# A four-layer graph transformer on one core: GpSimd issues the transfers of the inverse row sums

## Chip, cores and metric

The kernel runs on one core of one Trainium2 chip. The metric is the device time of one execution in microseconds (us); lower is better. Engines are called PE (TensorE), DVE (VectorE), ACT (ScalarE), POOL (GpSimd) and SP (the sync engine, which only issues transfers). DMA is a transfer between memories; it is issued by an instruction on SP or on POOL and ends, some time later, with a semaphore.

## What is computed

Four residual layers over `x` (8 batches, 1024 tokens, 256 features) and one adjacency matrix of 1024x1024. Layers 0 and 1 are graph convolutions. Layers 2 and 3 are attention with 8 heads of 32 features:

```python
# layer 2: mask is adj != 0; output projection, then o + layernorm(o)
attn = softmax(where(mask == 0, -inf, q @ k.T * scale))
o = (attn @ v) @ w_proj + b_proj
x = x + o + ln(o) * ln_gamma + ln_beta
# layer 3: (1 - adj) * -1e9 is added to the scores
attn = softmax(q @ k.T / sqrt(32) + (1 - adj) * -1e9)
x = x + (attn @ v) @ Wo + bo
```

`h = relu(layernorm(x))` feeds each layer. The kernel leaves the attention unnormalised until after the product with the values; only then does it multiply by the inverses of the row sums. Those inverses are what the change is about.

## The kernel before

**Phases.** `graph_phase` computes layers 0 and 1 (about the first 470 us). `attention_phase` computes layers 2 and 3: 16 jobs, one for each batch and layer (jobs 0 to 7 are layer 2, jobs 8 to 15 layer 3). A job has 64 units `u` (8 heads by 8 query tiles) and takes some 140 us. Each engine has a program of its own, written out by hand in the order in which the engine is to work; semaphores join them. While PE works on job n it also works off, in slots at fixed units, the end of job n-1 (table `EARLY`), the middle of job n (`MID`) and the beginning of job n+1 (`NEXT`).

**The four pairs of heads.** Two heads at a time share one output bank. For pair `pr` (0 to 3):

1. PE turns the row sums of 16 units (slot `norm`, L1047) and DVE takes their reciprocals into `rT`, 16x128 (L1399). The slots are at u=18, 33 and 48 for pairs 0, 1 and 2, and at u=1 of the following job for pair 3.
2. `write_rows` copies `rT` to the DRAM tensor `inverse_row_sums` (8 KB, L853). `read_rows` waits until that has landed and reads it back with 4 transfers, each repeated over 32 partitions, into `R_ot`, 128x512 (L859). Both are in SP's program. SP reaches them between `move_head` and `place_head` of heads 0, 2, 4 and 6: `move_head` sends a tile of probabilities to DRAM (L799) and `place_head` waits until it has landed and brings it back turned, with 4 transfers (L811).
3. ACT copies the output bank to `ot_sb` (L1260, semaphore `ot_done`).
4. POOL multiplies `ot_sb` by `R_ot` (`scale_ot`, L1656) once `ot_done` and `rows_in` say so, and issues 8 transfers to `oT_raw` (`regroup`, L1674).

**What follows on POOL.** POOL's program is `body` from L1718. Behind pair 3 of the job before come `move_v` (L1587), `bias_xe` (L1592) and `turn` (L1684, L1686), which splits a part of `oT_raw` for the output projection that PE does in the slots `out` at u=11, 15, 19 and 26 (L961 to L963 with `t_oT`). Behind `split(job, SPLITS[3])`, which follows the projection slot of u=22, come pair 0, then `bias_xe` of part 3 (needed by DVE's L1420 for the slot `out` 3 at u=26, in jobs 9 to 15 only), then `row_scale` (L1575, L1577, waits for the mean and variance that DVE makes in L1457), `norm` (L1623, L1626: four steps) and four splits of `h`. PE's slots `h` at u=34 and 35 (L1062) wait for `hn_done`, which L1626 counts: the one at u=34 for the second step, the one at u=35 for the fourth. Then come pair 1, `add_ln` of parts 2 and 3 (jobs 1 to 8), four splits, pair 2, and, in job 7 alone, `load_mask3` (L1712), which loads the mask of layer 3, needed by DVE's L1446.

Of the kernel before, what the change touches and what calls it, by code (L numbers as in the profile page):

```python
# [23 lines left out]
P = 128  # L24
# [512 lines left out]
def attention_phase(nc, a, x_mid, x_mid2, out, mask, shared, ident, PT, split, x_left, row_scratch, turned_rows, w_scratch):  # L537
# [11 lines left out]
    with ExitStack() as ctx:  # L549
# [199 lines left out]
        def _(sp):  # L749
# [95 lines left out]
            def write_rows(job, pr, key):  # L845

                pair = 4 * job + pr
                b, n = place[key]
                sp.wait_ge(bank_freed[b], n + 1)
                if pair:  # L850

                    sp.wait_ge(scaled, pair)
                sp.dma_start(row_scratch.rearrange("h (t q) -> (h t) q", q=P), rT[:]).then_inc(rows_out, 16)  # L853

            def read_rows(job, pr):

                sp.wait_ge(rows_out, 16 * (4 * job + pr + 1))
                for j in range(4):
                    sp.dma_start(R_ot[j * HD:(j + 1) * HD, :].rearrange("p (h t) -> p h t", h=2),  # L859
                                 row_scratch[:, 2 * j * P:2 * (j + 1) * P].partition_broadcast(HD)).then_inc(rows_in, 16)  # L860

            def body(job, layer, before, after):
                move_head(job, 0)
                if before is not None:
                    write_rows(job - 1, 3, key_of(job, ("norm", 3)))
                place_head(job, 0)
                if before is not None:
                    read_rows(job - 1, 3)
# [18 lines left out]
                write_rows(job, 0, key_of(job, ("norm", 0)))  # L887
                place_head(job, 2)
                read_rows(job, 0)
# [16 lines left out]
                write_rows(job, 1, key_of(job, ("norm", 1)))  # L906
                place_head(job, 4)
                read_rows(job, 1)
# [7 lines left out]
                write_rows(job, 2, key_of(job, ("norm", 2)))  # L916
                place_head(job, 6)
                read_rows(job, 2)
# [645 lines left out]
        def _(pool):  # L1564
# [85 lines left out]

            def scale_ot(job, pr):

                pair = 4 * job + pr
                pool.wait_ge(ot_done, pair + 1)
                pool.wait_ge(rows_in, 64 * (pair + 1))
                nc.gpsimd.tensor_tensor(ot_sb[:], ot_sb[:], R_ot[:], op=ALU.mult).then_inc(scaled, 1)  # L1656
# [61 lines left out]
            def body(job, layer, before, after):  # L1718
                if before is not None:
                    scale_ot(job - 1, 3)  # L1720
                    regroup(job - 1, 3)
# [20 lines left out]
                split(job, SPLITS[3])  # L1742
                scale_ot(job, 0)
# [5 lines left out]
                if after is not None:  # L1749
                    row_scale(job + 1)  # L1750
                    norm(job + 1)
                    for what in SPLITS[4:8]:
                        split(job, what)
                scale_ot(job, 1)
# [4 lines left out]
                if after is not None:  # L1759
                    for what in SPLITS[8:]:  # L1760
                        split(job, what)
                scale_ot(job, 2)
# [52 lines left out]
```

## Time and profile before

| | |
|---|---|
| median of 2 runs | 2754.8 us (2751.31 to 2758.28) |
| the profiled execution | 2757.91 us |
| its span, first to last instruction | 2756.0 us |
| granted TensorE clock, mean | 0.995 |
| PE busy | 2685.0 us, 97% of the span |
| DVE busy | 2238.5 us, 81% |
| ACT busy | 2022.5 us, 73% |
| POOL busy | 1384.9 us, 50% |
| DMA, mean over the span | 141 GB/s |

A busy time is the union of an engine's instructions. Idle time of an engine is put down to what ended it. The share says nothing of where a delay would hurt: an engine that is idle half the time can still be the one that another waits for at a given slot.

### The profile page before, as it was taken

To read this page: it belongs to the slowest core of one execution; us is meant where nothing else is said; L and a number is where in the kernel's file an instruction comes from. 1 tells how busy PE (TensorE), PEld (TensorE's weight loads), DVE (VectorE), ACT (ScalarE), POOL (GpSimd) and SP (SyncE) were. 2 spreads that over 40 slices of the span, in tenths; PEclk is the share of its full clock that TensorE was granted. 3 is DMA by queue.
4 is the path that set the end of the run, shared out by engine and by line. 5 is a ranking of instruction groups with operands and counts; after the bars stand their busy time and mean duration, and the time that the engine had idled before them with its cause. 6 is when DMAs were issued, how large, how long until landed. Compare 5 with 4: busy or idle time off the path is not lost.

```text
span 2756.0 us, 59363 instructions
## 1 busy us (share of the span) xinstructions
PE 2685.0 (97%) x22568; PEld 2113.3 (77%) x22568; DVE 2238.5 (81%) x4047; ACT 2022.5 (73%) x3680; POOL 1384.9 (50%) x1600
## 2 busy tenths in 40 slices
PE   9999999899999999999999999999999999999999
PEld 7888888677777777777777777777777777777776
DVE  6767676888888888888888888888888878887877
ACT  3000001888888888888888888888888888888887
POOL 2222221256767676767675758453535353536343
PEclk9999999999999999999999999999999999999999
DMA  3001001756665666665656675756565656665555
GB/s 134 31 31 62 30 32 41 186 154 163 158 162 156 163 160 159 157 156 151 170 142 175 162 195 142 188 144 172 143 178 136 174 147 166 156 159 153 158 145 138
DMA packets 433835, 387.62 MB, mean 141 GB/s; under 512 B 43520, under 2 KB 389872, under 8 KB 433552
## 3 DMA queue, kind: packets, MB, share of 16 engines
q1 hardware_dynamic: 416224, 362.94, 50.4%
q0 software_dynamic: 17328, 20.87, 2.9%
q8 instruction: 182, 2.98, 0.5%
q14 instruction: 101, 0.83, 0.1%
HBM read 139.07 MB, written 93.84 MB: 85 GB/s over the span
## 4 chain that ended last, share of the span: by engine, by line
PE 65%; POOL 7%; DMA 3%; SPq 2%; ACT 2%; issue 2%; DVE 2%; DVEq 0%; POOLq 0%; ACTq 0%
PE t_ring_ps L993 23%; PE t_ot_ps L1030 14%; PE t_s_ps L978 14%; PE t_ring_ps L961 4%; PE t_ring_ps L962 4%; PE t_ring_ps L963 4%; POOL t_oT_raw L1674 3%; DMA turned_rows<-t_turned_T 1%; DMA t_R_ot<-inverse_row_sums 1%; ACT t_T L1243 1%; PE t_ring_ps L1062 1%; POOL t_xe L1592 1%; POOL t_ot L1656 1%; SPq L811 1%; SPq L859 1%
## 5 line engine op out<-in xcount | busy, mean ns | idle before, releaser
L1341 DVE CUSTOM_DVE_ANT_0 t_T<-t_s_ps,mask 128x1024 f32<-128x1024 f32 x1024 | 1226.5, 1211 | 82.1 <-PE t_s_ps L978 76.8
L1243 ACT ACTIVATE t_T<-t_T,t_low 128x1024 f32<-128x1024 f32 x1024 | 1174.2, 1154 | 64.9 <-DVE t_low L1341 63.0
L993 PE MATMUL t_ring_ps<-ident,t_T 128*128 128x128 f32 x7184 | 967.1, 275 | 20.9 <-DVE t_xe L1420 12.6
L993 PEld LDWEIGHTS t_ring_ps<-ident,t_T 128*128 128x128 f32 x7184 | 826.5, 141 | 191.8 <-issue 61.3
L1251 ACT ACTIVATE PT<-t_ring_ps 128x512 f32<-128x512 f32 x1346 | 752.0, 598 | 217.6 <-PE t_ring_ps L993 211.0
L978 PE MATMUL t_s_ps<-t_k,t_q 128*128 128x512 f32 x2048 | 730.4, 438 | 3.5 <-DVE t_low L1341 3.3
L1030 PE MATMUL t_ot_ps<-PT,shared 128*32 128x256 f32 x8192 | 495.6, 382 | 7.0 <-DMA PT<-turned_rows 7.0
L1030 PEld LDWEIGHTS t_ot_ps<-PT,shared 128*32 128x32 f32 x8192 | 240.5, 109 | 232.5 <-issue 56.3
L1441 DVE COPY PT<-t_ring_ps 128x512 f32<-128x512 f32 x450 | 309.4, 687 | 101.7 <-PE t_ring_ps L993 97.8
L978 PEld LDWEIGHTS t_s_ps<-t_k,t_q 128*128 128x128 f32 x2048 | 310.0, 191 | 45.0 <-DVE t_low L1341 33.9
L273 ACT ACTIVATE g_yT_hi<-g_ps 128x512 fp32r<-128x512 f32 x64 | 38.3, 599 | 379.3 <-PE g_ps L205 379.3
L1647 POOL CAST t_st_hi<-t_st_lo 128x512 fp32r<-128x512 f32 x124 | 75.9, 612 | 395.4 <-DVE t_st_lo L1378 266.1
L1674 POOL DMA_DIRECT2D t_oT_raw<-t_ot x504 | 251.4, 506 | 26.4 <-POOL t_ot L1656 17.7
L1656 POOL TENSOR_TENSOR t_ot<-t_ot,t_R_ot 128x512 f32<-128x512 f32 x63 | 81.5, 1293 | 347.6 <-DMA t_R_ot<-inverse_row_sums 347.6
L1243 ACT ACTIVATION_READ_ACCUMULATOR t_T<-t_T,t_low 128x1 f32 x1024 | 205.4, 201 | 0.0
L1649 POOL TENSOR_TENSOR t_st_lo<-t_st_lo,t_st_hi 128x512 fp32r<-128x512 f32 x124 | 160.1, 1291 | 10.0
L1433 DVE STREAM_TRANSPOSE t_turned_T<-t_T 128x1024 f32<-128x1024 f32 x126 | 155.2, 1232 | 0.0
L305 POOL TENSOR_SCALAR g_var_eps<-g_mv 128x8 f32<-128x8 f32 x16 | 3.9, 241 | 259.0 <-DVE g_mv L352 259.0
L961 PE MATMUL t_ring_ps<-t_hT_hi,split 128*128 128x512 f32 x254 | 103.8, 409 | 0.3 <-DVE t_hT_lo L1353 0.3
L962 PE MATMUL t_ring_ps<-t_hT_lo,split 128*128 128x512 f32 x254 | 100.4, 395 | 0.0
L203 PE MATMUL g_ps<-g_adjT_hi,split 128*128 128x512 f32 x256 | 100.3, 392 | 0.1
L963 PE MATMUL t_ring_ps<-t_hT_hi,split 128*128 128x512 f32 x254 | 100.1, 394 | 0.0
(178 smaller groups left out, 3873.8 us busy)
## 6 DMA issues: line engine op xcount, KB each, us to landing
turned_rows<-t_turned_T SPq DMA_DIRECT2D x126, 512.0 KB, 3.4
PT<-turned_rows SPq DMA_DIRECT2D x504, 128.0 KB, 2.7
t_q<-t_st_hi SPq DMA_DIRECT2D x256, 128.0 KB, 2.3
t_q<-t_st_lo SPq DMA_DIRECT2D x256, 128.0 KB, 2.4
t_k<-t_st_hi SPq DMA_DIRECT2D x256, 128.0 KB, 2.4
t_k<-t_st_lo SPq DMA_DIRECT2D x256, 128.0 KB, 2.6
t_R_ot<-inverse_row_sums SPq DMA_DIRECT2D x252, 64.0 KB, 2.2
t_oT_raw<-t_ot POOLq DMA_DIRECT2D x504, 32.0 KB, 2.8
```

The source lines that it names most:

```text
L961: mm(dst, s_hi, m_hi, start=first, stop=False)
L962: mm(dst, s_hi, m_lo, start=False, stop=False)
L963: return mm(dst, s_lo, m_hi, start=False, stop=final)
L978: last = mm(s_ps[u % 2][:, cols], q4[h % 2][:, qt * P:(qt + 1) * P], k4[h % 2][:, cols], start=True, stop=True)
L993: last = nc.tensor.transpose(banks[b][:, i * P:(i + 1) * P], T[u % RING][:, kt * P:(kt + 1) * P], ident[:])
L1030: last = mm(ot_ps[j * HD:(j + 1) * HD, h % 2 * 2 * P:(h % 2 + 1) * 2 * P], v_sb[:, kt, h * HD:(h + 1) * HD], probs, start=kt == 0, stop=kt ...
L1243: nc.scalar.activation(T[u % RING][:], T[u % RING][:], ACT.Exp, bias=low[:, u % RING:u % RING + 1], scale=-1.0, accum_out=rsum[:, u:u + 1] ...
L1251: copy(pt_of(u, half), from_bank(banks[b], u), ACT.Copy).then_inc(bank_freed[b], 1)
L1341: nc.vector.tensor_tensor_reduce(out=T[u % RING][:], in0=s_ps[u % 2][:], in1=mask[:, qt, :], scale=1.0, scalar=3.4e38, op0=ALU.add, op1=AL ...
L1441: nc.vector.tensor_copy(pt_of(u, 1), from_bank(banks[b], u)).then_inc(bank_freed[b], 1)
L1649: nc.gpsimd.tensor_tensor(lo, raw_part, hi.bitcast(F32), op=ALU.subtract).then_inc(part_split, 1)
L1674: pool.dma_start(oT_raw[h % GH * HD:(h % GH + 1) * HD, h // GH, 2 * j * P:2 * (j + 1) * P], ot_sb[j * HD:(j + 1) * HD, 2 * hh * P:2 * (hh ...
```

## The change

The two helpers go from SP's program to POOL's, with `sp` replaced by `pool` and the same waits and semaphores. SP's five places lose them; in POOL's program they stand directly ahead of `scale_ot` of the same pair.

```diff
@@ sync engine
             def body(job, layer, before, after):
                 move_head(job, 0)
-                if before is not None:
-                    write_rows(job - 1, 3, key_of(job, ("norm", 3)))
                 place_head(job, 0)
-                if before is not None:
-                    read_rows(job - 1, 3)
...
                 move_head(job, 2)
-                write_rows(job, 0, key_of(job, ("norm", 0)))
                 place_head(job, 2)
-                read_rows(job, 0)
...
                 move_head(job, 4)
-                write_rows(job, 1, key_of(job, ("norm", 1)))
                 place_head(job, 4)
-                read_rows(job, 1)
...
                 move_head(job, 6)
-                write_rows(job, 2, key_of(job, ("norm", 2)))
                 place_head(job, 6)
-                read_rows(job, 2)
@@ GpSimd
+            def write_rows(job, pr, key):
+                pair = 4 * job + pr
+                b, n = place[key]
+                pool.wait_ge(bank_freed[b], n + 1)
+                if pair:
+                    pool.wait_ge(scaled, pair)
+                pool.dma_start(row_scratch.rearrange("h (t q) -> (h t) q", q=P), rT[:]).then_inc(rows_out, 16)
+
+            def read_rows(job, pr):
+                pool.wait_ge(rows_out, 16 * (4 * job + pr + 1))
+                for j in range(4):
+                    pool.dma_start(R_ot[j * HD:(j + 1) * HD, :].rearrange("p (h t) -> p h t", h=2),
+                                 row_scratch[:, 2 * j * P:2 * (j + 1) * P].partition_broadcast(HD)).then_inc(rows_in, 16)
...
                 if before is not None:
+                    write_rows(job - 1, 3, key_of(job, ("norm", 3)))
+                    read_rows(job - 1, 3)
                     scale_ot(job - 1, 3)
...
                 split(job, SPLITS[3])
+                write_rows(job, 0, key_of(job, ("norm", 0)))
+                read_rows(job, 0)
                 scale_ot(job, 0)
...
+                write_rows(job, 1, key_of(job, ("norm", 1)))
+                read_rows(job, 1)
                 scale_ot(job, 1)
...
+                write_rows(job, 2, key_of(job, ("norm", 2)))
+                read_rows(job, 2)
                 scale_ot(job, 2)
```

## Rows read from the trace of the kernel before

**Rows 1.** The page, part 1: busy time, share of the span, instructions
```profile
PE 2685.0 (97%) x22568; PEld 2113.3 (77%) x22568; DVE 2238.5 (81%) x4047; ACT 2022.5 (73%) x3680; POOL 1384.9 (50%) x1600
```
**Rows 2.** Waits: who waited for whom, us in total, times, longest us
```profile
PE t_ring_ps L961 <- POOL t_oT_lo L1686: 26.3, 14, 3.1
PE t_ring_ps L993 <- DVE t_xe L1420: 12.6, 7, 1.8
PE t_ot_ps L1030 <- DMA PT<-turned_rows: 7.0, 3, 3.1
...
POOL t_ot L1656 <- DMA t_R_ot<-inverse_row_sums: 347.6, 17, 24.5
```
**Rows 3.** DMA view: SP's write of the row sums, KB, median us to landing
```profile
inverse_row_sums<-t_rT SPq DMA_DIRECT2D x63, 8.0 KB, 1.4
```
**Rows 4.** Line L859 alone: us from issue to landing of its 252 transfers
```profile
DMA to landing us min/median/max: 1.9/2.2/4.5
```
**Rows 5.** Line L1674 alone: POOL's own issues (duration ns), and their landing
```profile
L1674 POOL DMA_DIRECT2D t_oT_raw<-t_ot x504: 496/496/767, 544.3 to 2727.1; - x168
...
DMA to landing us min/median/max: 1.6/2.8/6.6
```
**Rows 6.** Timeline of SP in job 10: start us, us, instruction
```profile
1940.91 0.32 SPq L853 DMA_DIRECT2D inverse_row_sums<-t_rT  x1
...
1943.22 3.22 SPq L859 DMA_DIRECT2D t_R_ot<-inverse_row_sums  x4
```
**Rows 7.** Timeline of POOL in job 10, pair 0 to the norm; brackets: idle before
```profile
1955.07 1.30 POOL L1649 TENSOR_TENSOR t_st_lo<-t_st_lo,t_st_hi 128x512 fp32r<-128x512 f32 x1
1956.31 1.30 POOL L1656 TENSOR_TENSOR t_ot<-t_ot,t_R_ot 128x512 f32<-128x512 f32 x1
1957.90 3.96 POOL L1674 DMA_DIRECT2D t_oT_raw<-t_ot  x8 [0.29 <-POOL t_ot L1656]
...
1965.66 0.25 POOL L1575 TENSOR_SCALAR t_var_eps<-t_mv 128x8 f32<-128x8 f32 x1 [2.51 <-DVE t_mv L1457]
```
**Rows 8.** Timeline of DVE, then of PE, in job 10 at u=26
```profile
1963.19 0.69 DVE L1420 TENSOR_TENSOR t_xe<-t_ring_ps,t_xe 128x512 f32<-128x512 f32 x1 [2.27 <-POOL t_xe L1592]
...
1964.03 1.06 PE L993 MATMUL t_ring_ps<-ident,t_T 128*128 128x128 f32 x8 [1.79 <-DVE t_xe L1420]
```
**Rows 9.** Timeline of POOL, then of PE, in job 3 around the slots h
```profile
969.67 0.25 POOL L1575 TENSOR_SCALAR t_var_eps<-t_mv 128x8 f32<-128x8 f32 x1 [1.30 <-DVE t_mv L1457]
...
979.24 1.04 POOL L1626 TENSOR_TENSOR shared<-shared,t_rstd 128x512 f32<-128x512 f32 x1
...
981.80 0.60 PE L1062 MATMUL t_ring_ps<-ident,shared 128*128 128x128 f32 x4
```
**Rows 10.** The same three in job 0
```profile
550.06 0.24 POOL L1575 TENSOR_SCALAR t_var_eps<-t_mv 128x8 f32<-128x8 f32 x1 [1.53 <-DVE t_mv L1457]
...
559.62 1.04 POOL L1626 TENSOR_TENSOR shared<-shared,t_rstd 128x512 f32<-128x512 f32 x1
...
565.08 0.61 PE L1062 MATMUL t_ring_ps<-ident,shared 128*128 128x128 f32 x4
```
**Rows 11.** Timeline of SP, then of POOL, between jobs 2 and 3 (pair 3)
```profile
911.64 0.32 SPq L853 DMA_DIRECT2D inverse_row_sums<-t_rT  x1
...
917.83 1.28 POOL L1656 TENSOR_TENSOR t_ot<-t_ot,t_R_ot 128x512 f32<-128x512 f32 x1 [19.86 <-DMA t_R_ot<-inverse_row_sums]
```
**Rows 12.** The same between jobs 3 and 4
```profile
1050.61 0.32 SPq L853 DMA_DIRECT2D inverse_row_sums<-t_rT  x1
...
1057.74 1.29 POOL L1656 TENSOR_TENSOR t_ot<-t_ot,t_R_ot 128x512 f32<-128x512 f32 x1 [20.79 <-DMA t_R_ot<-inverse_row_sums]
```
**Rows 13.** Timeline of POOL and DVE in job 7; line L1712 alone: landing
```profile
1606.15 1.12 POOL L1712 DMA_DIRECT2D mask<-in_adj  x2
...
1612.69 0.77 DVE L1446 TENSOR_SCALAR mask<-mask 128x1024 f32<-128x1024 f32 x1
...
DMA to landing us min/median/max: 3.8/6.3/15.6
```

More of the change, by code:

```diff
@@ L843, in load_tail_weights @@
                                      w_scratch[part][2 * HD:, 1, 3 * D:].rearrange("(h d) o -> d h o", d=HD)).then_inc(w_tail_in, 16)
[L845 to L860, printed above, removed]
             def body(job, layer, before, after):
                 move_head(job, 0)
-                if before is not None:
-                    write_rows(job - 1, 3, key_of(job, ("norm", 3)))
                 place_head(job, 0)
-                if before is not None:
-                    read_rows(job - 1, 3)
                 load_head(job, 2, UNITS * job + 8, None)
```

## Prediction

> **What bounds the kernel.** I read the page's busy shares first: PE works through 97% of the span, so only 3% is left for it to gain, and any pause that it is given adds to the end [rows 1]. Then the waits. PE's longest ones all concern the end of a job: 26.3 us in 14 waits for POOL's last split of `turn`, in front of the slot `out` 0, and 12.6 us in 7 waits behind DVE's L1420. POOL waits 347.6 us for the rows, but in 17 waits only: at most 24.5 us each [rows 2]. There are 15 job ends, and two more pairs in the last job with nothing for POOL to do before them: those are the 17. The other 46 of the 63 scalings found their rows there already. That is the question of this case: where does POOL reach the transfers early and sit idle anyway, and where does it reach them late, so that a round trip to DRAM that used to run beside its work now stands in it? The timelines answer it pair by pair.
>
> **What is removed from SP.** 63 writes and 252 reads. SP bounds nothing of size: PE waits for one of its transfers 7.0 us in 3 waits [rows 2]. I put the gain from a shorter SP queue at 0. Its bounds are 0 and 7.
>
> **What a round trip costs POOL.** Call D the time from POOL's reaching `write_rows` to its reaching `scale_ot`. The trace has no row transfer issued by POOL; the nearest row is its own `regroup`: 0.50 us for an issue, landing after 1.6 at the least, 2.8 in the median, 6.6 at the most [rows 5]. SP's own figures are 1.4 for the write [rows 3] and 1.9, 2.2 and 4.5 for the reads [rows 4].
>
> - write, until it lands: 1.6 (regroup's least) to 2.8 (its median). It is small and alone on its queue, so I take the middle, 2.2;
> - the semaphore waits ahead of the reads and of the scaling: 0.3 and 0.1, after the 0.29 that POOL sat idle between scaling and regroup [rows 7];
> - three of the four reads are issued ahead of the last: 3 x 0.5 = 1.5;
> - the last read lands: 1.9 (SP's least) to 4.5 (SP's most). I take regroup's median 2.8, since SP sends head tiles at the same time.
>
> D = 2.2 + 0.3 + 1.5 + 2.8 + 0.1 = 6.9 us. With the least values it is 1.6 + 0.2 + 1.5 + 1.9 + 0.1 = 5.3, with the most 2.8 + 0.3 + 1.5 + 4.5 + 0.1 = 9.2.
>
> By the Trainium skill (DMA: Bandwidth & Descriptors, Anatomy of one DMA — SWDGE path) a transfer that GpSimd issues takes some 2.0 us plus its bytes over 436 GB/s, which would be 2.0 and 2.2 for these two, an estimate of D = 6.1, and an end of 2817 by the sum below. Of the regroup, of 32 KB, the trace shows 1.6 to 6.6 around a median of 2.8, so I stay above the page.
>
> **Pair 0, jobs 9 to 15.** In job 10 SP wrote at 1940.91 and read from 1943.22, 3.22 us of issues [rows 6]. POOL came to the scaling at 1956.31, straight from its split, without a wait [rows 7]. Now the trip starts there. Behind it, in order, are the scaling, 8 regroups, `bias_xe` of part 3, `row_scale` and `norm`. DVE's L1420 waits for that bias already (2.27 us) and PE behind it (1.79) [rows 8], seven times in the trace [rows 2]. There is no slack: each of the 7 jobs pays D on PE. The norm of these jobs waits for a mean that DVE makes behind L1420 (2.51 us idle, [rows 7]), so it moves along with PE and costs nothing more.
>
> **Pair 0, jobs 0 to 8.** Nobody waits for that bias here; what is late next is `norm`, then PE's slot `h` at u=35, which needs the fourth step. In job 3 POOL idled 1.30 ahead of `row_scale`, the last step ended at 980.28 and PE took it up at 981.80, 1.52 later: slack 2.8 [rows 9]. In job 0 it is 1.53 + (565.08 - 560.66 = 4.42) = 5.9 [rows 10]. Seven jobs I count like job 3 and two (0 and 7, which looks alike) like job 0: 7 x 2.8 + 2 x 5.9 = 31.4. These nine jobs pay 9D - 31.4.
>
> **Pairs 1 and 2.** POOL is late by D as well: behind pair 2 it used to idle some 20 us until the next rows [rows 11, 12], and behind pair 1 comes `add_ln`, whose results go to stores, and four splits whose inputs ACT and DVE make only 12 units after the `norm` slot. Hidden, at 0; if the cover behind pair 1 fell short by 1 us in the 8 jobs with `add_ln`, it would be 8 us.
>
> **Pair 3, 15 job ends.** POOL stands idle here (19.86 and 20.79 us), so it issues the moment the reciprocal is done. From SP's write to the scaling it was 917.83 - 911.64 = 6.2 and 1057.74 - 1050.61 = 7.1, with SP's four reads of turned tiles in between [rows 11, 12]; I take 6.7 for the fifteen. D against 6.7 is +0.2, 15 x 0.2 = +3. PE waits right behind this, so it is felt, but a gain can't exceed PE's 26.3 us of waiting [rows 2].
>
> **Once: job 7.** The first mask tile is issued at 1606.15, behind regroup 2, and used at 1612.69; a mask load lands in 6.3 in the median, so hardly any slack; the least is 3.8 [rows 13]. POOL comes D later: between 6.54 - 6.3 and 6.54 - 3.8 of it is covered, leaving 4 to 7 us. The write of pair 3 then queues behind eight mask loads on POOL's own queue. I take 5.
>
> **Sum.** 7D + 9D - 31.4 = 16 x 6.9 - 31.4 = 79; + 3 + 5 = 87 us. PE at 97% leaves nothing in which a pause could be recovered; I take off 2. Profiled execution 2757.9 + 85 = 2843. The median shown lies 3.1 below that execution: 2840 us, 3.1% slower. Each microsecond of D is worth 31 us of the end.
>
> **Rivals.**
>
> 1. *The forecast*, D between 6 and 8: 16D - 31.4 + 15(D - 6.7) + 5 is 59 to 121, so 2814 to 2876.
> 2. *A short trip*, D near 5.3: 53 - 21 (job ends gain) + 5 = +37, 2792. For it: an undisturbed regroup lands in 1.6. Against: it needs the least value at both landings in every job.
> 3. *A long trip*, D over 8: 9.2 gives 116 + 37 + 5 = +158, 2913. For it: SP issues head tiles in the same microseconds, and its four reads in job 10 took 3.22 rather than 1.86 [rows 6]. A form of it is that DVE holds GpSimd's port: the Trainium skill (SBUF — State Buffer, SBUF: two separate sides) says that GpSimd can't write descriptors while VectorE runs certain instructions. The 504 regroup issues took 496 to 767 ns with the median at 496 [rows 5], which speaks against it. At 0.5 us more for each of 5 issues, D would be 9.4 and the end 2919.
> 4. *Only layer 3 pays*: the norm's slack in jobs 0 to 8 holds more than I see. 7 x 6.9 + 3 + 5 = 56, 2811, on the 2% line.
> 5. *Not slower*: the job ends are the place. SP's queue holds the row reads behind four others there, POOL frees them, and PE gets its 26.3 us back, which with nothing lost at pair 0 is 2729. It decides as soon as 16D - 31.4 is under 26.3, that is D under 3.6. Against: three issues and two landings of 1.6 and 1.9 are already 5.0.
>
> **Chances.** Forecast 0.60, short trip 0.17, long trip 0.14, only layer 3 0.05, not slower 0.04. The range goes from 2792 (rival 2) to 2885 (D = 8.3: 101 + 24 + 5 = +130), leaving out rival 5 and most of 3. Two per cent, about what this kernel's measurement tells from no change, is 2810: slower by over 2% gets all of the forecast and of rival 3 with parts of 2 and 4, 0.79; within 2% gets most of 2, half of 4 and half of 5, 0.18; faster 0.03. What is within 2% is on the slow side, mostly.
>
> **What would show it.** POOL: the wait in front of L1656 at all 63 scalings, not 17, with three to four microseconds of it behind the reads and about two ahead of them, and some 315 more issues of 0.5 us. DVE: L1420's wait for L1592 in jobs 9 to 15 at 2.3 + D = 9.2 us instead of 2.3. PE: 1.8 + D behind it; and new waits of L1062 for L1626 of about 4 us in jobs 1 to 8. L961's wait for L1686 stays near 2 us. I am wrong if D comes out under 5.3, if PE's new idle time is much under 80 us, or if L1062 doesn't wait.

## The result, and the profile after

| | before | after |
|---|---|---|
| median of 2 runs | 2754.8 us | 2939.2 us (2936.3 to 2942.1) |
| span of the profiled execution | 2756.0 us | 2934.5 us |
| PE busy | 2685.0 us | 2731.8 us |
| PE idle, span less busy | 71.0 us | 202.7 us |
| granted TensorE clock, mean | 0.995 | 0.969 |

The ratio is 1.0669, with a 95% interval of 1.0651 to 1.0686. The kernel became 6.7% slower. The direction was forecast; the size was not: 184 us instead of 85, and 2939 us lies 54 us above the upper end of the range.

The busy shares come first, against [rows 1]. The page of the changed kernel:

```profile
PE 2731.8 (93%) x22568; PEld 2141.7 (73%) x22568; DVE 2241.0 (76%) x4047; ACT 2027.6 (69%) x3680; POOL 1553.9 (53%) x1915
```

POOL has 315 instructions more (63 writes, 252 reads). PE has none more, but is busy for 46.8 us more and idle for 131.7 us more. These two are the whole 178.5 us between the spans. The lines of the code have moved up by 27 or 10: L993 is now L966, L1420 L1393, L1592 L1565, L961 L934, L1062 L1035, L1626 L1599, L1341 (DVE's pass over the scores) L1314, L1378 (DVE's raw copy into the staging tile `st_lo`) L1351, L1656 L1646, the reciprocal L1399 L1372; the write is L1632, the reads L1638.

Who waited for whom in the changed kernel (waiter, awaited, us in total, times, longest us):

```profile
PE t_ring_ps L966 <- DVE t_xe L1393: 72.0, 7, 12.0
PE t_ring_ps L934 <- POOL t_oT_lo L1676: 37.0, 14, 5.4
PE t_ring_ps L1035 <- POOL shared L1599: 34.9, 17, 4.7
PE t_ring_ps L966 <- DVE t_st_lo L1351: 19.1, 8, 4.2
PE t_s_ps L951 <- DVE t_low L1314: 11.0, 6, 7.7
...
DVE t_xe L1393 <- POOL t_xe L1565: 75.4, 7, 12.5
...
POOL t_ot L1646 <- DMA t_R_ot<-inverse_row_sums: 176.3, 63, 6.4
POOL inverse_row_sums L1632 <- DVE t_rT L1372: 125.4, 17, 16.3
POOL t_R_ot L1638 <- DMA inverse_row_sums<-t_rT: 113.1, 63, 3.3
...
POOL t_oT_raw L1664 <- issue: 15.4, 7, 2.5
...
SPq L786 <- POOL t_xe L1589: 79.5, 9, 11.8
```

POOL now waits for the rows at all 63 scalings, 17 before [rows 2], and as often for its own write. The first row is the pause of layer 3: 12.6 us in 7 waits before, 72.0 now, with DVE and POOL behind it. The third is PE at the slots `h`; before, PE waited for that line not once. The fourth row, of 19.1 us in 8 waits, belongs to no step of the forecast. In the fifth PE waits behind DVE, once for 7.7 us, where it is the mask of job 7; in the kernel before this wait was 3.3 us in 5.

Timeline of POOL in job 9 of the changed kernel, pair 0 (start, us, instruction; in brackets the idle time before it):

```profile
1904.11 0.52 POOL L1632 DMA_DIRECT2D inverse_row_sums<-t_rT  x1
1906.02 0.55 POOL L1638 DMA_DIRECT2D t_R_ot<-inverse_row_sums  x1 [1.40 <-DMA inverse_row_sums<-t_rT]
1907.83 1.60 POOL L1638 DMA_DIRECT2D t_R_ot<-inverse_row_sums  x3 [1.26 <-issue]
1912.65 1.26 POOL L1646 TENSOR_TENSOR t_ot<-t_ot,t_R_ot 128x512 f32<-128x512 f32 x1 [3.21 <-DMA t_R_ot<-inverse_row_sums]
1914.20 3.99 POOL L1664 DMA_DIRECT2D t_oT_raw<-t_ot  x8 [0.29 <-POOL t_ot L1646]
1918.20 1.27 POOL L1565 TENSOR_TENSOR t_xe<-t_xe,t_row_bias 128x512 f32<-128x512 f32 x1
```

D, from the write's start to the scaling's, is 1912.65 - 1904.11 = 8.54 us here. Over the sixteen pairs 0 it is 8.3 in the mean (6.8 to 10.8). The sixteen writes landed after 2.2 in the mean and the last of the four reads after 4.0.

The same place as PE sees it, in the changed kernel:

```profile
1909.43 0.60 PE L966 MATMUL t_ring_ps<-ident,t_T 128*128 128x128 f32 x4
1920.35 1.94 PE L966 MATMUL t_ring_ps<-ident,t_T 128*128 128x128 f32 x8 [10.32 <-DVE t_xe L1393]
```

And in windows of 7 us (PE, PEld, DVE, ACT and POOL busy, PEclk, share of the DMA engines, GB/s):

```profile
1905.00:1912.00 7.00, 5.03 (x42) 4.18 (x34) 3.70 (x7) 4.94 (x10) 2.15 (x4) 1.00 0.75 192
1912.00:1919.00 7.00, 0.00 (x0) 0.00 (x0) 0.00 (x0) 0.00 (x0) 6.04 (x10) 0.52 0.53 150
1919.00:1926.00 7.00, 5.65 (x41) 3.49 (x42) 3.62 (x13) 4.47 (x8) 4.25 (x5) 0.51 0.00 0
1926.00:1933.00 7.00, 7.00 (x72) 5.51 (x68) 6.00 (x10) 5.10 (x10) 6.37 (x7) 1.00 0.59 131
```

PE stood still for 10.32 us. In its second window the granted clock is 0.52, and it is still 0.51 when PE works again: half of full speed, that is 1.2 instead of 2.4 GHz. Eight transposes took 1.94 us there, and 1.06 before the change, at the same slot of job 10 [rows 8]. So a pause costs more than its length. This is where PE's 46.8 us of additional busy time come from: after the change PE was at work for 116.8 us in stretches of the lower clock, before it for 23.6, and half of the difference is 46.6.

**Where the time sits.** DVE takes a reciprocal at every slot `norm` (u=18, 33, 48, and u=1 of the next job). The time between one reciprocal and the next, less that of the kernel before, summed over the jobs:

| stretch | after, us | in which jobs |
|---|---|---|
| u=18 to 33 | +75.3 | 9 to 15, 10.7 each |
| u=33 to 48 | +50.2 | 0 to 8, 5.6 each |
| u=48 to 1 | +37.6 | 7 (14.2); the others of 1 to 8 together 23 |
| u=1 to 18 | +15.7 | the job ends |

The sum with the -0.3 ahead of the first reciprocal is 178.5. The experiments are told by the same four stretches, in this order.

### The profile page after: what moved, and what is told of

It reads as the page before. It is cut to its first block, busy times and chain, and to the rows that moved or that the text cites. A ratio compares the mean times of both kernels' runs of the same rounds, so it can differ in the third digit from the quotient of the medians.

```text
span 2934.5 us, 59363 instructions
## 1 busy us (share of the span) xinstructions
PE 2731.8 (93%) x22568; PEld 2141.7 (73%) x22568; DVE 2241.0 (76%) x4047; ACT 2027.6 (69%) x3680; POOL 1553.9 (53%) x1915
## 4 chain that ended last, share of the span: by engine, by line
PE 50%; POOL 18%; DMA 8%; issue 3%; ACT 2%; DVE 2%; SPq 2%; DVEq 0%; POOLq 0%; ACTq 0%
PE t_ring_ps L966 18%; PE t_ot_ps L1003 11%; PE t_s_ps L951 10%; POOL t_oT_raw L1664 5%; DMA t_R_ot<-inverse_row_sums 4%; PE t_ring_ps L934 3%; PE t_ring_ps L936 3%; PE t_ring_ps L935 3%; DMA inverse_row_sums<-t_rT 3%; POOL t_R_ot L1638 2%; POOL t_ot L1646 2%; POOL t_st_lo L1622 1%; SPq L768 1%; POOL shared L1599 1%; POOL shared L1596 1%
## 5 line engine op out<-in xcount | busy, mean ns | idle before, releaser
L1314 DVE CUSTOM_DVE_ANT_0 t_T<-t_s_ps,mask 128x1024 f32<-128x1024 f32 x1024 | 1227.2, 1212 | 95.6 <-PE t_s_ps L951 90.2
L966 PE MATMUL t_ring_ps<-ident,t_T 128*128 128x128 f32 x7184 | 986.4, 279 | 99.1 <-DVE t_xe L1393 72.0
L966 PEld LDWEIGHTS t_ring_ps<-ident,t_T 128*128 128x128 f32 x7184 | 842.7, 143 | 272.4 <-issue 119.1
L951 PE MATMUL t_s_ps<-t_k,t_q 128*128 128x512 f32 x2048 | 740.9, 443 | 11.2 <-DVE t_low L1314 11.0
L1003 PE MATMUL t_ot_ps<-PT,shared 128*32 128x256 f32 x8192 | 507.5, 389 | 7.4 <-DMA PT<-turned_rows 7.4
L1664 POOL DMA_DIRECT2D t_oT_raw<-t_ot x504 | 251.6, 506 | 34.1 <-POOL t_ot L1646 18.5
L1638 POOL DMA_DIRECT2D t_R_ot<-inverse_row_sums x252 | 135.7, 545 | 114.5 <-DMA inverse_row_sums<-t_rT 113.1
L1646 POOL TENSOR_TENSOR t_ot<-t_ot,t_R_ot 128x512 f32<-128x512 f32 x63 | 80.9, 1284 | 176.3 <-DMA t_R_ot<-inverse_row_sums 176.3
L934 PE MATMUL t_ring_ps<-split,t_oT_hi 128*128 128x256 f32 x240 | 73.0, 304 | 38.4 <-POOL t_oT_lo L1676 37.0
L934 PE MATMUL t_ring_ps<-t_hT_hi,split 128*128 128x512 f32 x254 | 103.8, 408 | 0.3 <-DVE t_hT_lo L1326 0.3
L1351 DVE TENSOR_SCALAR t_st_lo<-t_ring_ps,t_b_qk 128x512 f32<-128x512 f32 x46 | 34.4, 748 | 89.7 <-PE t_ring_ps L936 63.5
```

Source lines behind the costliest of these rows:

```text
L934: mm(dst, s_hi, m_hi, start=first, stop=False)
L951: last = mm(s_ps[u % 2][:, cols], q4[h % 2][:, qt * P:(qt + 1) * P], k4[h % 2][:, cols], start=True, stop=True)
L966: last = nc.tensor.transpose(banks[b][:, i * P:(i + 1) * P], T[u % RING][:, kt * P:(kt + 1) * P], ident[:])
L1003: last = mm(ot_ps[j * HD:(j + 1) * HD, h % 2 * 2 * P:(h % 2 + 1) * 2 * P], v_sb[:, kt, h * HD:(h + 1) * HD], probs, start=kt == 0, stop=kt ...
L1314: nc.vector.tensor_tensor_reduce(out=T[u % RING][:], in0=s_ps[u % 2][:], in1=mask[:, qt, :], scale=1.0, scalar=3.4e38, op0=ALU.add, op1=AL ...
L1638: pool.dma_start(R_ot[j * HD:(j + 1) * HD, :].rearrange("p (h t) -> p h t", h=2), row_scratch[:, 2 * j * P:2 * (j + 1) * P].partition_broa ...
```

## The experiments

Theory A is: what costs is that a trip to DRAM stands between POOL and its next work. The main rivals: GpSimd's issuing costs by itself (in POOL's time, or in what it disturbs), SP's queue is what changes, or the size of a trip differs by place. "Rival B" in the expectations is one form or another of the first of them. "Against the kernel before" is the kernel before on the same chip, 2751.8 to 2754.7 us. In the kernels in which both queues issue trips, each queue has semaphores of its own.

### One pair at a time

In each kernel only one of the four pairs' trips goes to GpSimd; for pair 0:

```diff
@@ sync engine
                 move_head(job, 2)
-                write_rows(job, 0, key_of(job, ("norm", 0)))
                 place_head(job, 2)
-                read_rows(job, 0)
@@ GpSimd
+                write_rows(job, 0, key_of(job, ("norm", 0)))
+                read_rows(job, 0)
                 scale_ot(job, 0)
```

> Only pair 0's transfers are issued by GpSimd; pairs 1, 2 and 3 stay on the sync engine, with counters of their own. Theory A (the place decides): pair 0 carries the loss. Between the norm slots of pairs 0 and 1 the changed kernel is 75.3 us longer (all of it in jobs 9 to 15), between those of pairs 1 and 2 50.2 us (jobs 0 to 8). So +115 to +130 us, 2870 to 2885, with DVE's wait for the bias of part 3 at about 75 us in 7 waits, and the stretches from u=48 to the end of the job as before. Rival B (a transfer issued by GpSimd costs the same wherever it stands): a quarter of 184, +46, 2801.

> Only pair 1's transfers are issued by GpSimd. Theory A: in jobs 1 to 8 the layer norm behind pair 1 ends later, SP's store of part 2 and the head-7 load behind it start later, and DVE's raw copy at u=49, which may only overwrite what head 7 was loaded from, waits. In the changed kernel the stretches from u=48 on are 23 us longer in those jobs (job 7's mask aside): +15 to +25 us, none in jobs 9 to 15. Rival B: +46. The prediction's own reading (hidden): 0 to +8.

> Only pair 2's transfers are issued by GpSimd. Theory A: POOL is idle behind pair 2 in all jobs but job 7, where the mask load of layer 3 is late: +5 to +14 us, once. Rival B: +46.

> Only pair 3's transfers are issued by GpSimd. Theory A: POOL stands idle before them and a round trip of 6 to 8 us takes the place of one of 6.7 from the reciprocal to the scaling: +5 to +16 us, all between the norm slots of pairs 3 and 0 (changed kernel: +15.7 there). Rival B: +46. If SP's queue was what held the job ends: a gain, down to -26.

| pair issued by GpSimd | median, us | over before | ratio, interval | the four stretches |
|---|---|---|---|---|
| 0 | 2881.6 | +127 | 1.0458, 1.0443 to 1.0474 | +78.2, +49.4, 0, -5.1 |
| 1 | 2783.1 | +29 | 1.0100, 1.0085 to 1.0115 | +3.6, -0.3, +24.9, -4.3 |
| 2 | 2773.2 | +19 | 1.0061, 1.0046 to 1.0076 | +2.5, -0.3, +7.2 (all in job 7), +4.4 |
| 3 | 2793.5 | +39 | 1.0142, 1.0125 to 1.0160 | u=1 to 18: +30.0 |

Pair 0 is the mass of it, in just the two stretches that the forecast named, and only there did the expectation hold. Pair 1, put down as hidden, costs 29 where 15 to 25 were expected; pair 2 costs 19 (expected 5 to 14) and pair 3 costs 39 (expected 5 to 16). The four add to 214, above the 184 of all together. They don't simply add; pair 3 is a part of that, with 30.0 us in its stretch here and 15.7 in the changed kernel. Its waits in the kernel that moves only pair 3:

```profile
PE t_ring_ps L967 <- POOL t_oT_lo L1713: 44.2, 14, 7.2
```

That is 17.9 us over [rows 2]. D of pair 3 was 7.7 us there against 6.7 before, and the write landed after 2.7 in the mean, 1.75 for SP's in the kernel before. With every trip on GpSimd it was 6.8. Why GpSimd's write of pair 3 is slower while SP still issues the others isn't settled.

### Issues without a trip

The order of before; SP does every trip, but POOL also issues five idle transfers (one of 8 KB, four of 16 KB; the real reads bring 64 KB each) ahead of pair 0's scaling, and waits for none of them in the same job:

```diff
+                idle_transfers(job)     # one of 16 x 128, four of 32 x 128, ident to a scratch tensor
                 scale_ot(job, 0)
```

> The kernel before, with five transfers more that GpSimd issues ahead of the scaling of pair 0 and that nothing waits for (8 KB and four times 16 KB, on-chip to a spare DRAM tensor; the real row transfers stay on the sync engine). It prices the issues without the round trip. Theory A (the round trip is the price, not the issues): POOL comes 5 x 0.5 = 2.6 us later to the scaling; jobs 9 to 15 pay that each, 18 us, jobs 0 to 8 have 2.8 us of slack or more and pay nothing: +15 to +25. Rival B (issuing from GpSimd is the price, through a shared port or its queue): near pair 0's whole 127 us.

2792.7 us, 1.0137 (1.0122 to 1.0153): +38, where theory A expected 15 to 25 and rival B near 127. Five issues took 1 x 0.60 + 4 x 0.50 = 2.6 us of POOL. PE's waits in this kernel:

```profile
PE t_ring_ps L994 <- DVE t_xe L1421: 30.5, 7, 5.0
```

30.5 - 12.6 = 17.9 us over [rows 2], or 2.6 in each of the seven jobs: exactly POOL's issuing. Yet the jobs 9 to 15 became longer by 4.9 each. The other half is PE's busy time, 2701.4 instead of 2685.0 us: pauses of at most 5.0 us already cost clock. Jobs 0 to 8 paid 1 us together, since 2.6 fits into the slack of 2.8 that [rows 9] gave.

### Only the reads on GpSimd

SP writes pair 0's rows at the old time, GpSimd reads them ahead of the scaling:

```diff
@@ sync engine
                 place_head(job, 2)
-                read_rows(job, 0)
@@ GpSimd
+                read_rows(job, 0)
                 scale_ot(job, 0)
```

> Pair 0's write stays on the sync engine, GpSimd issues only its four reads. Theory A: the trip at pair 0 is shorter by the write's landing and its wait, 8.3 - 2.5 = 5.8 us. By the prediction's own form, 7 x 5.8 + (9 x 5.8 - 31.4) = 61, with pauses that are shorter and so lose less clock: +60 to +90, where pair 0 alone was +127. Rival B (the reads, which are four of the five, carry all of it): +110 or more.

2833.7 us, 1.0289 (1.0274 to 1.0305), stretches +55.6 and +26.2. So the reads alone cost 79 of pair 0's 127 us, and the write on top of them 48. Neither is small.

### Keeping PE busy in the pause

On the changed kernel, PE does 72 idle transposes into a bank that is free ahead of the slot `out` 3 of layer 3:

```diff
+                    if what == ("out", 3) and before == 1:
+                        b, n = place["B", job, u]
+                        pe.wait_ge(bank_freed[b], n)
+                        for _ in range(72):
+                            nc.tensor.transpose(banks[b][:, 0:P], ident[:], ident[:])
```

> The changed kernel, with 72 idle 128x128 transposes on PE directly ahead of the block out 3 in jobs 9 to 15 (7 places). They take 72 x 0.11 = 7.9 us each time, less than the some 10 us for which PE goes idle behind that block anyway, and write into a bank that is free and overwritten after them. Theory A (part of the loss is the clock): the changed kernel's PE is granted half its clock in a stretch around every one of these pauses (0.51 from 1919 to 1926 us), so with PE kept at work the 7 stretches stay at full clock and some 2 us come back at each: 10 to 20 us faster than the changed kernel, 2920 to 2930. Rival B (the lower clock falls only on idle time and costs nothing): no change, or up to 10 us slower, since the fill stands ahead of work that was done before the pause.

2926.7 us, 1.0620 (1.0604 to 1.0636), 12.5 under the changed kernel. The stretch u=18 to 33 of jobs 9 to 15 fell from 75.1 to 64.2 over the kernel before, and the mean clock rose from 0.969 to 0.981. The same windows of this kernel:

```profile
1912.00:1919.00 7.00, 7.00 (x67) 6.32 (x60) 3.91 (x7) 3.95 (x8) 2.14 (x4) 1.00 0.71 192
1919.00:1926.00 7.00, 6.12 (x54) 5.74 (x51) 0.00 (x0) 1.20 (x2) 6.18 (x10) 1.00 0.54 150
```

POOL's trip is as long as before (D is 8.0 us in the mean of these seven jobs in both kernels), and PE's own work waits for it as long as before: in job 9 the idle transposes took 8.02 us and the wait left behind them 2.10, beside the one wait of 10.32. But PE is at work and its clock stays at 1.00. So 11 of the 75 us there are shown to be the clock's. Not all of it came back: PE's busy time there had grown by 15.6. The rest is the pause.

### Another order behind the trip

On the changed kernel, the bias goes ahead of the trip (`bias_first`); or it goes between write and reads, and the norm between reads and scaling (`trip_under_norm`):

```diff
+                if before is not None:
+                    bias_xe(job - 1, before, XE)
                 write_rows(job, 0, key_of(job, ("norm", 0)))
                 read_rows(job, 0)
                 scale_ot(job, 0)
                 regroup(job, 0)
-                if before is not None:
-                    bias_xe(job - 1, before, XE)
```

```diff
                 write_rows(job, 0, key_of(job, ("norm", 0)))
-                read_rows(job, 0)
-                scale_ot(job, 0)
-                regroup(job, 0)
                 if before is not None:
                     bias_xe(job - 1, before, XE)
+                read_rows(job, 0)
...
                     norm(job + 1)
+                scale_ot(job, 0)
+                regroup(job, 0)
```

> The changed kernel, with the bias of part 3 moved ahead of the row transfers of pair 0 in POOL's program. Theory A: DVE's L1420 no longer waits behind the round trip, so the 75.3 us of jobs 9 to 15 go, and PE's old 1.8 us there too (12.6). What is left in those jobs is the norm: 8.3 us late against 4.8 of slack, 3 to 4 us each, some 25. Jobs 0 to 8 as in the changed kernel. 2939 - 75 - 12 + 25 = 2877; range 2860 to 2890. Rival (the norm, not the bias, holds those jobs): 2920 or more.

> The changed kernel with pair 0's trip laid under other work of POOL: write, bias of part 3, reads, row_scale and norm, and only then scaling and regroup. GpSimd still issues all the transfers. Theory A: everything that the changed kernel loses from u=18 to u=48 goes (75.3 and 50.2 us), and PE's old wait of 1.8 us in jobs 9 to 15 with it (13): 2939 - 75 - 50 - 13 = 2801, range 2790 to 2812. Rival B (issuing from GpSimd costs by itself): no better than 2877, the kernel with the bias first.

`bias_first`: 2877.5 us (1.0432, 1.0403 to 1.0461), stretches -13.0 and +83.2. Layer 3's pause is gone, and so is the 13 us that [rows 8] had there before. But the jobs 9 to 14 now pay as the others do, at the norm (job 15 has no job behind it): their norm used to wait for a mean behind the bias; with that early, it waits for POOL. The cost moved one slot on.

`trip_under_norm`: 2816.7 us (1.0240, 1.0225 to 1.0256), stretches -14.0, +29.3, +25.1, +19.1. It is 123 us under the changed kernel, with the same 63 trips by the same queue, and 5 above the range that was expected. It is the place of a trip that costs. The +29.3 is looked at below.

### add_ln ahead of pair 1

```diff
+                if before == 0:
+                    add_ln(job - 1, 2)
+                    add_ln(job - 1, 3)
                 write_rows(job, 1, key_of(job, ("norm", 1)))
                 read_rows(job, 1)
                 scale_ot(job, 1)
                 regroup(job, 1)
-                if before == 0:
-                    add_ln(job - 1, 2)
-                    add_ln(job - 1, 3)
```

> The changed kernel with the two layer norms (add_ln of parts 2 and 3, jobs 1 to 8) moved ahead of pair 1's row transfers. Theory A: SP's store of part 2 and the head-7 load behind it are no longer held, so DVE's wait for a transfer at u=49 (26.1 us in 8 waits) and 23 of the 37.6 us from u=48 on go; job 7's 14 stay: 2910 to 2920. Rival (those 23 us come from pair 2's trip): no change, 2939.

2907.7 us (1.0566, 1.0548 to 1.0583), 32 under the changed kernel and 2 under the expected range. The stretch u=48 to 1 fell from +37.6 to +9.6, and all that is left of it is job 7. PE's wait for L1351 is gone with it. The chain that it cuts, in job 2 of the changed kernel, seen on SP and then on DVE:

```profile
895.09 0.38 SPq L786 DMA_DIRECT2D x_after_layer<-t_xe  x1
895.51 1.62 SPq L768 DMA_DIRECT2D t_q<-t_st_hi  x2
...
900.50 0.60 SPq L768 DMA_DIRECT2D t_k<-t_st_lo  x1
901.20 0.53 SPq L799 DMA_DIRECT2D turned_rows<-t_turned_T  x1
```

```profile
903.00 0.75 DVE L1351 TENSOR_SCALAR t_st_lo<-t_ring_ps,t_b_qk 128x512 f32<-128x512 f32 x1 [5.07 <-DMA t_k<-t_st_lo]
```

`add_ln` comes late, so SP's store of its result comes late. SP works in order: the loads of the next head, whose data are long there, stand behind the store. DVE may not overwrite the staging tile `st_lo` before those loads have read it, and waits 5.07 us. PE waits for DVE: the fourth row of the waits above. That a store has nobody waiting for it says nothing of what is queued behind it.

### All trips covered, first attempts

`all_covered` joins the above (pair 3's scaling behind `move_v` and the first bias, pair 0's behind the norm, `add_ln` and the mask loads ahead of the scalings they followed). `all_covered2` has pair 0's scaling two splits further on:

```diff
                     norm(job + 1)
+                if after is not None:
+                    for what in SPLITS[4:6]:
+                        split(job, what)
                 scale_ot(job, 0)
                 regroup(job, 0)
```

> GpSimd issues all row transfers, each trip laid under work that POOL has anyway: pair 0 under bias and norm, pair 1 under the layer norms, the mask of layer 3 loaded ahead of pair 2's write, and at job ends move_v and the first bias between the reads and the scaling. Theory A: no loss is left and PE's waits at u=26 (13 us) and part of those at job ends (26 us plus clock) go: 2715 to 2740, faster than both kernels. Rival B (issuing from GpSimd costs by itself): over 2770.

> all_covered with one order changed: the first two splits of h stand ahead of pair 0's scaling and regroup instead of behind them. Theory A (the 29.4 us that all_covered still loses between u=33 and 48 are these splits, for which ACT waits before it may overwrite the raw tile): they go, 2765 - 29 = 2736, range 2730 to 2745, faster than the kernel before though GpSimd issues every transfer. Rival B (GpSimd's issuing costs what remains): no change, 2765.

2765.1 us (1.0053, 1.0038 to 1.0068), stretches -12.5, +29.4, +1.7, -10.3; and 2880.2 us (1.0454, 1.0436 to 1.0472). Both missed: the first lies 25 us above its range of 2715 to 2740, the second 144 above the 2736 that were expected.

### The new order with SP, and with one pair moved

`b_reordered` is the kernel before, SP issuing every trip, with two moves in POOL's program:

```diff
-                if before is not None:
-                    scale_ot(job - 1, 3)
-                    regroup(job - 1, 3)
                 move_v(job)
...
                     bias_xe(job - 1, before, 0)
+                    scale_ot(job - 1, 3)
+                    regroup(job - 1, 3)
                     turn(job - 1, 0)
...
-                scale_ot(job, 0)
-                regroup(job, 0)
                 if before is not None:
                     bias_xe(job - 1, before, XE)
+                scale_ot(job, 0)
+                regroup(job, 0)
```

`pair0_covered` gives pair 0 of it to GpSimd, with the late scaling of `all_covered2`. `pair3_covered` gives it pair 3, issued ahead of `move_v`.

> The kernel before (the sync engine issues), with two orders of POOL changed: the bias of part 3 ahead of pair 0's scaling, and at job ends move_v and the first bias ahead of pair 3's scaling. Theory A: 13 us at u=26 and 15 to 30 us at the job ends: 2712 to 2730. Rival (PE's waits there are only moved elsewhere): 2745 to 2755. Against all_covered it tells whether who issues matters once every trip is covered: within 10 us of it by theory A.

> b_reordered (2709 us), with pair 0's transfers issued by GpSimd and their trip laid under bias, norm and the first two splits of h. Theory A: the place that cost +127 us when the trip stood bare costs 0 to 5 us covered: 2707 to 2716. Rival B: a cost of its own of 16 trips, over 2725.

> b_reordered (2709 us), with pair 3's transfers issued by GpSimd, move_v and the first bias between the reads and the scaling. Here no work can cover the trip: it begins when the reciprocal is done and PE waits for its end. Theory A: what is left of GpSimd's disadvantage is the trip's own length, 0.3 to 1.5 us at each of 15 job ends and the clock behind the longer pauses: +10 to +30, 2719 to 2739. Rival B (equal in length to the sync engine's trip, as predicted): 2704 to 2714.

`b_reordered`: 2709.3 us, 0.9845 (0.9831 to 0.9860), faster than both kernels and 3 us under the expected range; PE busy 2675.3 us, 99% of the span. It takes away the two waits of PE that [rows 2] began with: stretches -9.7, 0, -0.1, -38.1. `all_covered` was expected within 10 us of it and lies 56 above.

`pair3_covered`: 2734.8 us (0.9926, 0.9907 to 0.9945), 26 above it, as expected. At a job end POOL has nothing to put over the trip but `move_v` and one bias, 2.3 us together.

`pair0_covered`: 2867.6 us (1.0405, 1.0385 to 1.0426), 158 above it where 0 to 5 were expected, all of it in the stretch u=33 to 48, some 10.5 us in each of 15 jobs. Its waits of PE and ACT, and ACT's timeline in job 4:

```profile
PE t_ring_ps L1070 <- ACT PT L1259: 124.9, 15, 8.6
```

```profile
ACT t_ot L1268 <- DMA t_oT_raw<-t_ot: 130.4, 15, 9.0
```

```profile
1161.34 0.21 ACT L1251 ACTIVATION_READ_ACCUMULATOR t_T<-t_T,t_low 128x1 f32 x1
1170.34 0.60 ACT L1268 ACTIVATE t_ot<-t_ot_ps 128x512 f32<-128x512 f32 x1 [8.80 <-DMA t_oT_raw<-t_ot]
```

ACT copies pair 1's outputs into `ot`, which must have been emptied by pair 0's regrouping. With that delayed, ACT stands for 8.80 us, its later copies of `PT` are late, and PE finds no free bank. In `all_covered` the same ACT row is 30.7 us in 14 waits, its +29.4; in `trip_under_norm`, with its +29.3, 24.4 in 13; in `all_covered2` 121.5 in 16; in `b_reordered` ACT's list of waits has no such row. So the loss of these kernels looks like that of a late scaling, not of a trip. This was read from traces only after they had run. The next three runs test it from one side, by leaving the scaling where it was; no run delays the scaling with SP issuing the trips.

### All trips covered, without delaying a scaling

The order of `b_reordered` is kept exactly. Only the trip goes earlier in POOL's program, into places where POOL stood idle:

```diff
                 split(job, SPLITS[0])
                 if before is not None:
                     turn(job - 1, 3)
+                write_rows(job, 0, key_of(job, ("norm", 0)))
                 split(job, SPLITS[1])
+                read_rows(job, 0)
                 split(job, SPLITS[2])
                 split(job, SPLITS[3])
                 if before is not None:
                     bias_xe(job - 1, before, XE)
                 scale_ot(job, 0)
```

> GpSimd issues the round trip of pair 0 alone; the kernel is b_reordered (2709.3 us) in all else, and nothing of its order of scaling, regrouping, norm and splits is changed. The write stands ahead of the split of SPLITS[1], where POOL of b_reordered idled 2.3 to 3.6 us, the reads ahead of SPLITS[2], where it idled 2.0 us; the scaling follows 5.1 us behind the last read. Theory A (what costs is only that the trip stands between POOL and its next work; the loss of pair0_covered is ACT's copy_ot that waits for the late regroup of pair 0): 2709 to 2716. Rival B (transfers that GpSimd issues cost in themselves, about 5 us a job in jobs 9 to 15 as in issues_only, or the 10.5 us a job of pair0_covered): 2744 or 2867.

> As early0, and pairs 1 and 2 the same way: pair 1's write and reads stand behind SPLITS[5] (POOL idled 4.2 us there; write landing 2.2 and reads 2.2, so 0.2 us late at most), pair 2's write behind SPLITS[9] (idle 3.3), its reads behind SPLITS[10] (idle 2.0). Only pair 3 stays with SP. Theory A: 2709 to 2722, with no wait of DVE for the head's loads (the +25 us of pair1_only gone). Rival B: each pair adds its issues, 3 x 16 x 2.7 us = up to 130 us, where add_ln and the splits are late.

> As early012, and pair 3 issued by GpSimd ahead of move_v, as in pair3_covered (which was 26 us above b_reordered). All 64 round trips are then GpSimd's, and SP has none, as in the changed kernel. Theory A: early012 plus 20 to 30 = 2730 to 2750, below the first kernel's 2753. Rival B: 2860 or more.

| GpSimd issues | median, us | ratio, interval |
|---|---|---|
| none (`b_reordered`) | 2709.3 | 0.9845, 0.9831 to 0.9860 |
| pair 0 | 2712.7 | 0.9843, 0.9821 to 0.9865 |
| pairs 0, 1, 2 | 2719.6 | 0.9868, 0.9842 to 0.9893 |
| all four | 2735.0 | 0.9922, 0.9894 to 0.9950 |

Timeline of POOL in job 10 of `early0`:

```profile
1922.90 0.51 POOL L1670 DMA_DIRECT2D inverse_row_sums<-t_rT  x1
1926.60 0.61 POOL L1658 CAST t_st_hi<-t_st_lo 128x512 fp32r<-128x512 f32 x1 [3.19 <-DVE t_st_lo L1386]
1927.30 1.28 POOL L1660 TENSOR_TENSOR t_st_lo<-t_st_lo,t_st_hi 128x512 fp32r<-128x512 f32 x1
1928.54 2.18 POOL L1676 DMA_DIRECT2D t_R_ot<-inverse_row_sums  x4
...
1935.83 1.31 POOL L1685 TENSOR_TENSOR t_ot<-t_ot,t_R_ot 128x512 f32<-128x512 f32 x1
```

The write lands under an idle stretch of 3.19 us, the reads under two splits and the bias, and the scaling has no idle time before it. The same five transfers per job that cost 127 us directly ahead of the scaling cost nothing that these runs can tell from 0. All three times lie where theory A put them. Pairs 1 and 2 add 7 us (in the trace 4.8 in job 7 and 4.5 in job 13, less 5 elsewhere), and pair 3 adds 15. With all 63 trips on GpSimd the kernel is 0.8% faster than the one before, but that gain is the new order's: with SP issuing in the same order it is 26 us faster still.

The page of that last kernel:

```profile
PE 2679.1 (98%) x22568; PEld 2109.4 (77%) x22568; DVE 2239.4 (82%) x4047; ACT 2020.7 (74%) x3680; POOL 1550.9 (57%) x1915
```

POOL has as many instructions and as much busy time as in the changed kernel, 1550.9 against 1553.9 us. Only places in POOL's program differ, and they are worth 204 us. Of these, some 45 are what the new order brought with SP as well (`b_reordered` against the kernel before). The other 158 or so are the trips' own: against SP in the same order they cost 184 us directly ahead of the scalings and 26 in their early places.

## Why the prediction was wrong in size

**What held.** The bound (PE), the one question (where POOL reaches the transfers late), and the two places: jobs 9 to 15 through L1420 and the bias, jobs 0 to 8 through the norm. `pair0_only` put 128 us into just these two stretches, which also rules out rival 4 (only layer 3 pays); a D of 8.3 rules out rivals 2 and 5. The forecast sum, read for PE's idle time alone, was 85 us plus a clock term of 0. Three steps of it failed: the clock had no term, pair 1 was taken as hidden, and the last read was taken as too short. PE's waits, the measured ones less those of the kernel before:

| PE waits for | forecast, us | measured, us |
|---|---|---|
| L1393, pair 0 in jobs 9 to 15 | 7D = 48 | 72.0 - 12.6 = 59.4 |
| L1599, pair 0 in jobs 0 to 8 | 9D - 31.4 = 31 | 34.9 |
| L1676, job ends | 3 | 37.0 - 26.3 = 10.7 |
| L1314, the mask of job 7 | 5 | 11.0 - 3.3 = 7.7 |
| L1351, pair 1 in jobs 1 to 8 | 0 | 19.1 |
| sum | 87, less 2 | 131.8 |
| PE's additional busy time, the clock | 0 | 46.8 |

The two sums of the right column, 178.6, are the whole difference of the spans, 178.5.

**The clock had no term at all.** "PE at 97% leaves nothing in which a pause could be recovered" is true, and says nothing of what a pause does to PE afterwards. PE's 46.8 us of additional busy time are a quarter of the loss. The trace of before held the warning only in small: short pauses and a clock of 0.995. By the Trainium skill (TensorE: Matmul & The Clock Gate, HAM oscillation — how this bites in real kernels) half of the time spent throttled is lost; worked out from the mean clocks that would be an estimate of 0.031 x 2934.5 - 0.005 x 2756.0 = 77 us. The trace shows 47, since some of the throttled time is that of the pause itself, in which PE had no work to slow (the window 1912 to 1919): the lower clock lasted 184.7 us, and PE was at work in 116.8 of them.

**Pair 1 was hidden at 0 (bound 8) and cost 23.** The step followed who reads `add_ln`'s result, a store, and stopped there. It did not go on to what stands behind that store on SP's queue. `add_ln_first` took 28 us from this stretch, `pair1_only` brought 25.

**D was 6.9 and is 8.3.** The write was sized right (2.2 taken, 2.2 measured). The failed term is the last read, with 1.2 of the 1.4: 2.8 taken, from regroup's median, 4.0 measured at pair 0 (3.2 to 6.8). In other places the same read landed after 2.6 (pair 1), 3.7 (pair 2) and 2.4 (pair 3). SP's head tiles were named as the reason to go above regroup's least, and then regroup's median was still too little. By the trace's packets the DMA engines were busy for 80% of the time of this read at pair 0 and 75% at pair 2, and for 66 and 57% at pairs 1 and 3, so the long landings go with the busier engines; no run tests that. DVE was busy for some 60% of this read at pair 0 and over 90% of it at the others, which speaks against DVE as the cause. In jobs 9 to 15, D was 8.0 and PE paid it in full. In jobs 0 to 8 it was 8.5, 77 us in nine jobs, and PE's waits were 35: the slack is some 42 us there, not 31.4. So the long D was partly made up for by a second mis-sized term, which is luck. `issues_only` shows only that the slack is about 2.6 or more.

Rival 3, a long trip (D over 8), was the nearer case, though its 2913 us was still too little. The upper end of the range, 2885, was worked out for just the D of 8.3 that came, so the 54 us above it are not D's: they are above all the clock and pair 1. The cause that the forecast gave for one form of rival 3, slower issuing, did not come: L1632 and L1638 took 0.59 and 0.54 us in the median, beside regroup's 0.50.

**The mask of job 7: 5 forecast, 7.7 of waiting and 14 in all measured** for that job's stretch. The eight loads landed after 9.4 us in the median instead of 6.3 [rows 13], and DVE waited 7.62 us for the first. POOL's being late by D at pair 2 was priced; that the loads themselves would be slower was not. `pair2_only` shows 7.2, so the rest came from the other moves; with `add_ln` ahead of pair 1, 9.7 of the 14 stay.

**Pair 3: 3 forecast, 16 measured** in the job-end stretch: PE's wait there grew by 10.7, from 26.3 to 37.0, and its busy time by 4.8. The wait comes apart in three. D there was 6.8 as against 6.7 before, which is the forecast's own term, and explains 1.4 us in the fifteen job ends. GpSimd's write began 0.29 us after the reciprocal, SP's 0.03: 3.9 us. And in two of the job ends POOL stood for 2.5 us in the middle of the eight transfers of its regroup (two of the seven waits of L1664 for "issue" above): 5 us. What such a stop is isn't known; the kernel before has three of them in regroup, none at a job end. `pair3_only` cost more (39) than this place does in the full change, which stays open.

**What the text said would show it.** All 63 scalings wait: yes, 176.3 / 63 = 2.8 us behind the reads and 113.1 / 63 = 1.8 ahead of them, a little under the three to four and the two that were named. L1393's wait for L1565 would be 9.2 us each: 75.4 / 7 = 10.8, and PE's behind it 8.7: 72.0 / 7 = 10.3. L1035 would wait about 4 us in jobs 1 to 8: 34.9 in 17 waits, at most 4.7. L934's wait would stay: it grew from 1.9 to 2.6 us each. None of the three signs of being wrong came; they were chosen against a smaller loss, not against a larger one.

## What to carry to other kernels

When a transfer moves to a queue that also computes, first ask where in that engine's program its latency would lie under work or idle time, and put each step of it there; here the same 63 trips cost 184 us directly ahead of their consumer and 26 in early places, each against SP in the same order. Price a new pause of TensorE above its length: the work right behind the pause can run at half clock, as eight transposes did here with 1.94 us for 1.06. And follow a late result past its reader: to what is queued behind the store on its in-order queue, and to the buffer that a late step fails to empty.

## What was unexpected in the hardware

- **A pause's second price.** In seven jobs PE's pause grew by 2.6 us and the job by 4.9 (`issues_only`); with 10 us pauses, eight transposes behind one took 1.94 us where they had taken 1.06. Idle transposes in seven such pauses brought 11 us back.
- **The last of four reads of 64 KB issued by GpSimd** landed 4.0 us after its issue in the mean at one place in the program and 2.4 at another (pair 0 and pair 3 of the changed kernel), with the same size and shape. At pair 0 its write landed after 1.6 at the least and 2.2 in the mean, SP's in the kernel before after 1.3 and 1.7.
- **GpSimd's issuing is cheap, but now and then it stops**: 0.50 to 0.59 us in the median for each plain two-dimensional transfer, and 5 per job cost nothing that could be measured where POOL would have idled. Six times in the changed kernel POOL stood for 2.5 us between two transfers of a regroup and once for 1.3 between two reads, and the profile shows nothing that it waited for.
